# One clip operation per step instead of three in the deformable loop of a four-layer network

## The reference

```python
x = x + _L0_conv_ref(_gn(x), ...)   # spectral convolution
x = x + _L1_conv_ref(_gn(x), ...)   # convolution, times a matrix, batch norm
x = x + _L2_conv_ref(_gn(x), ...)   # deformable convolution, batch norm
x = x + _L3_conv_ref(_gn(x), ...)   # 3x3 convolution
```

```python
def dsc_axis(x, offset, weight, axis):
    ...
    if axis == 'x':
        ix = wb + off
        iy = jnp.broadcast_to(hb, off.shape)
    ...
    s = grid_sample_zeros(x, ix, iy)      # linear interpolation, zero outside
    return jnp.einsum('bchwk,ock->bohw', s, weight)
```

## Time and profile before

| | |
|---|---|
| median of 3 runs | 4393.8 us |
| the profiled execution's own time | 4387.39 us |
| its span, first to last instruction | 4385.3 us |
| `deformable`, first `apply` to last | 1904.5 to 4101.7 us of the span |
| busy in the whole span | PE 83%, ACT 60%, DVE 58%, POOL 56% |
| granted TensorE clock, mean of the span | 0.901 of 2.4 GHz |

### The profile page before, as it was taken

One profiled execution on the slowest core, in us unless ns is written; L12 is line 12 of the kernel. 1 busy time (PEld: TensorE's weight loads), 2 busy tenths in 40 slices (PEclk: granted clock), 3 DMA queues, 4 the chain that ended last, 5 costly groups with the idle time before them and its releaser, 6 DMA issues. The chain is left out here.

```text
span 4385.3 us, 142489 instructions
## 1 busy us (share of the span) xinstructions
PE 3644.4 (83%) x59682; PEld 2156.9 (49%) x59682; DVE 2559.5 (58%) x5104; ACT 2639.7 (60%) x2951; POOL 2443.9 (56%) x1787
## 2 busy tenths in 40 slices
PE   6866548723799996569999999999999999999588
PEld 5755444423233332246655556555565555655222
DVE  5401646633233335757777777777777777776555
ACT  5600103323122225469999989999899999998442
POOL 0010220001000004769999999999999999999500
PEclk9955658955899998879999999999999999999799
DMA  3264649999877776532221221212212122020585
GB/s 99 58 136 117 193 113 238 222 322 279 198 219 216 216 212 260 190 83 59 57 69 45 68 59 35 69 45 68 59 35 69 45 66 59 17 71 22 137 211 125
DMA packets 675526, 532.88 MB, mean 122 GB/s; under 512 B 39434, under 2 KB 600714, under 8 KB 667050
## 3 DMA queue, kind: packets, MB, share of 16 engines
q1 hardware_dynamic: 556444, 386.26, 34.1%
q10 hardware_dynamic: 108560, 105.02, 7.8%
q0 software_dynamic: 9984, 33.56, 2.3%
HBM read 338.51 MB, written 186.19 MB: 120 GB/s over the span
## 5 line engine op out<-in xcount | busy, mean ns | idle before, releaser
L1563 POOL TENSOR_SCALAR df_t<-df_t 128x1536 f32<-128x1536 f32 x1536 | 2200.0, 1570 | 51.3 <-ACT df_t L1573 51.2
L1744 PE MATMUL df_o<-df_t,df_zs 128*32 128x128 f32 x36864 | 1326.8, 277 | 42.6 <-POOL df_t L1563 27.9
L1616 DVE TENSOR_SCALAR df_t<-df_d 128x512 int32<-128x512 int32 x1536 | 1062.6, 692 | 487.8 <-PE df_d L1700 483.6
L1573 ACT ACTIVATE df_t<-df_a 128x1024 f32<-128x1024 f32 x1024 | 1051.7, 1027 | 204.4 <-PE df_a L1700 201.9
L1744 PEld LDWEIGHTS df_o<-df_t,df_zs 128*32 128x32 f32 x36864 | 914.1, 109 | 470.7 <-issue 263.8
L1700 PE MATMUL df_d<-df_ix,net_sel 11*128 11x512 bf16 x1536 | 592.7, 386 | 2.5 <-DVE df_t L1616 0.9
L1573 ACT ACTIVATE df_t<-df_z 128x1024 f32<-128x1024 f32 x512 | 525.8, 1027 | 36.3 <-PE df_z L1700 5.4
L1577 ACT ACTIVATE df_zs<-df_z 128x864 f32<-128x864 f32 x512 | 452.9, 884 | 2.0 <-PE df_z L1724 2.0
L1700 PE MATMUL df_a<-df_ix,net_sel 11*128 11x512 bf16 x2048 | 398.3, 386 | 46.7 <-DMA df_ix<-offset 46.6
L1724 PE MATMUL df_z<-net_Z,df_x 32*128 32x288 f32 x4096 | 393.2, 429 | 18.0 <-ACT df_x L1591 9.6
L1089 POOL CAST of_parts<-of_t_o 128x512 bf16<-128x512 f32 x64 | 64.0, 1000 | 615.6 <-ACT of_t_o L1066 586.8
(11 more groups left out here) (228 smaller groups left out, 4749.2 us busy)
## 6 DMA issues: line engine op xcount, KB each, us to landing
gc_x<-x SPq DMA_DIRECT2D x240, 128.0 KB, 4.8
dc_x<-x SPq DMA_DIRECT2D x240, 128.0 KB, 3.3
dc_xt<-x_2t SPq DMA_DIRECT2D x240, 128.0 KB, 4.7
fw_x<-in_x SPq DMA_DIRECT2D x32, 512.0 KB, 6.7
iv_x<-in_x SPq DMA_DIRECT2D x64, 256.0 KB, 4.7
x<-iv_x POOLq DMA_DIRECT2D x64, 256.0 KB, 5.0
y<-gc_o ACTq DMA_DIRECT2D x64, 256.0 KB, 5.5
r_y<-y SPq DMA_DIRECT2D x8, 2048.0 KB, 13.8
```

The lines of the kernel that those rows point to most:

```text
L1563: g.tensor_scalar(t, t, 1.0, 0.0, ALU.min, ALU.max).then_inc(hat_p, 1)
L1573: act.activation(T[:, n % 2, 3 * i:3 * i + 2], src, ACT.Abs).then_inc(a_read, 1)
L1616: v.tensor_scalar(T[:, n % 2, 3 * i + 2].bitcast(I32), ps_d[:].bitcast(I32), 0x7fffffff, None, ALU.bitwise_and).then_inc(d_read, 1)
L1744: mm = pe.matmul(ps_o[32 * q:32 * q + 32, 0:P], Zs[:, n % 2, q, 32 * k:32 * k + 32], T[:, n % 2, 3 * i + x, P * q:P * q + P], start=(k == ...
```

## The change

The clip of a step becomes one operation over all nine tiles, 4608 columns, in place of three over 1536. It waits until all three groups of distances of the step have been written, and `hat_p` counts steps, not groups; every `apply` of a step waits for the same count.

```diff
             @block.gpsimd
             def _(g):
                 for n in range(ST):
-                    for i in range(3):
-                        g.wait_ge(a_read, 3 * n + i + 2)
-                        g.wait_ge(d_read, 3 * n + i + 2)
-                        t = T[:, n % 2, 3 * i:3 * i + 3].rearrange("p k n -> p (k n)")
-                        g.tensor_scalar(t, t, 1.0, 0.0, ALU.min, ALU.max).then_inc(hat_p, 1)
+                    g.wait_ge(a_read, 3 * n + 4)
+                    g.wait_ge(d_read, 3 * n + 4)
+                    t = T[:, n % 2].rearrange("p k n -> p (k n)")
+                    g.tensor_scalar(t, t, 1.0, 0.0, ALU.min, ALU.max).then_inc(hat_p, 1)
...
-                    pe.wait_ge(hat_p, 3 * n + i + 1)
+                    pe.wait_ge(hat_p, n + 1)
                     for x, k in enumerate((2 * i, 2 * i + 1, 6 + i)):
```

## The result

The changed kernel takes 4498.16 us (median of 4 runs, 4489.94 to 4508.85), the kernel before 4392.16 us in runs on the same chip. The ratio is 1.024, 95% interval 1.021 to 1.0271: 2.4% slower. I had predicted 4483 us.

The account below looks back on a forecast made before the run. A chain over two steps replaces full POOL as bound: 256 x 4.39 + 256 x 4.515 = 2279.7 us against 2199.6, +80; irregular steps bring +89; 4393.8 + 89 = 4483 us, range 4450 to 4545.

Parts of the forecast that it names:

- the ring: Loop chain over two steps, apply, spread, distance, clip, apply: 8.78 us in row phases, 9.03 in column phases; chance 0.88.
- The links of the ring: Row phase: 3.12 to last spread, 0.43 to distance, 1.03 distance, 0.08 to POOL, 4.07 clip, 0.05 to apply, in us.
- Apply to last distance: From first apply of step n to the end of the last distance of n + 2, across spreads and ACT's distance.
- my lower end: Lowest estimate for the 4608-column clip on POOL: 0.833 ns a column from two plain fills, 4.02 us.
- The irregular steps: Loop steps with `line_totals` and the `read_s` wait, 15 x 0.5 = +7 us, and the low-clock first round, +2 us.
- The sum: +80 us from the ring and +9 us from the irregular steps: +89 us on the profiled execution's 4387.4.
- PE's waits: PE should wait for POOL only before a step's first apply, 0.2 to 0.3 us.
- half a turn apart: Even and odd steps each have a ring, offset so that PE's 4.12 and POOL's 4.07 us pass without conflict.
- Faster: Rival: POOL stays the bound at 4.04 us a step, then PE decides: -75 us, 4319 us; chance 0.05.
- The clock rival: More PE idle time lowers the granted clock in the loop: 5% of steps +31 us, all +600; chance 0.04.

Follow-up runs that it names:

- the two conditions: Kernel before, three clips: each clip waiting for all three distances, 4391.21 us; or each apply waiting for all three clips, 4392.42 us.

## Why the prediction was right, point by point

- *The bound moves from POOL to the ring.* Right: POOL idle in front of its clips, released by ACT, and the two conditions harmless alone.
- *The links of the ring.* Apply to last distance was put at 4.58 and 4.83 us; the trace of the changed kernel has 4.57 and 4.83, and 0.08 from ACT to POOL, as was forecast. With the clip and the next link that is 4.57 + 0.08 + 4.03 + 0.15 = 8.83 and 9.09, the rings measured. The clip was put at 4.07 and takes 4.03, 0.837 ns a column over the short one: the plain fill's price, my lower end, was the nearer row. That is -10 us.
- *The link that was mis-sized* is "its end to the next apply ... 0.05 us". It takes 0.146 us, (0.146 - 0.05) / 2 x 512 = +25 us. The row that I used shows the apply of group 2, which has one wait in front. Of the first applies of a step the trace of before holds nearly none that wait for a clip.
- *The irregular steps.* +9 us predicted; beyond its rings (256 x 4.415 + 256 x 4.545 = 2293.8) the loop took 6.4. The step with `line_totals` cost about 0.7 us in a row phase and 0.2 in a column phase, not 0.5 in each, and the last step at the lower clock, 1.3 us, was not in the forecast.
- *The sum.* 89 us predicted, +14 for the rings (25 - 10, and under 1 for the rest), -3 for the irregular steps, and 2.4 because the loop before measures 2197.2 us by its timeline and not the 2199.6 of 512 equal steps: 103, the difference measured. The forecast was 15 us low in the median. The link alone would have made it some 10 us worse; the clip, put too high, hid that by luck.
- *PE's waits* came in front of the first apply alone, but not 0.2 to 0.3 us at each: steps of 4.21 and 4.62 us alternate in row phases, so every second one has 0.5 of wait and the other 0.1 beyond PE's 4.12. The text had the rings half a turn apart; nothing fixes their offset. PE's busy time was to stay near 2143 us and is 2181; what makes up these 38 us was not followed up, and matmul ends are modelled in the profile.
- *Rivals.* Faster was out as reckoned. The sizes given for it were slightly wrong: with the links of the forecast (8.78 - 4.07 = 4.71 and 9.03 - 4.07 = 4.96) the clip would have to be under 8.59 - 4.71 = 3.88 and 3.63 us, not 3.92 and 3.67, or 0.79 and 0.71 ns a column, which makes the case against it stronger. The Trainium skill's two sentences (Perfetto Trace Analysis, Optimizing Scalar/DVE Operations), larger operations where an engine is saturated and smaller ones where they cause bubbles, both held here, though they speak of other engines: from the kernel before, with POOL full, 3072 columns in one operation gained 25 us; from the changed kernel, with POOL idle in front of its clips, breaking the 4608 columns into 3072 and 1536 took 4498 us to 4365. The clock rival failed: with PE busy 94.8% of the loop the granted clock fell in the last step alone, which cost 1.3 us.
- *Not tested:* a third buffer for `T`, which would spread the same ring over three steps.

## What to carry to other kernels

A full engine has two numbers, the time of its operations and the slack of the rings that pass through it. Before merging operations, add up the ring from the release of a buffer to its next use and divide by the number of buffers; if that exceeds the step, as here, the merge loses, whatever fixed parts it saves. The ring grew so long only because the clip both started late and released late; a merge that leaves part of the work able to start and release early kept the gain, here with 3072 + 1536 columns: 4365 us, against 4390 before and 4498 changed. And look for the next engine before promising the whole gain, as 25 of 55 us came.

## What the runs showed of the hardware that was not expected

- A wait put last of four in front of a matmul group cost 0.146 us from the clip's end to the matmul, the same wait put first 0.054. Which part of the waiting takes the 0.09 us was not tested.
- POOL's clip costs 1.46 us at 1536, 2.75 at 3072, 3.60 at 4096 and 4.03 at 4608 columns: 0.837 ns a column and a fixed part of about 0.17 us, of which about 0.15 us remain when operations follow each other back to back (1.432 - 1536 x 0.837 ns = 0.146).
